# Four images through a four-layer network: LSTMs in pairs of images, all sampling moved behind the first pair

## The reference

```
x = x + L0(gn(x))   # attention of 8x8 blocks over 14x14 halo windows, 4 heads
x = x + L1(gn(x))   # LSTM, 128 hidden, along the 96 columns of each of the 96 rows; then a linear map to 32 channels
x = x + L2(gn(x))   # deformable 3x3 convolution: 9 bilinear samples per pixel at learned offsets, masked, convolved
x = x + L3(gn(x))   # each 8x8 block multiplied from both sides by one 8x8 matrix
```

## Time and profile before

| | us |
|---|---|
| three runs | 5402.57, 5425.98, 5408.45 (median 5408.45) |
| the profiled execution | 5414.31 |
| its span (first to last instruction) | 5412.5 |

### The profile page before, as it was taken

How to read it: one execution, slowest core, us unless ns; L and a number is a source line. 1 busy time by engine, 2 the same in 40 slices (tenths; PEclk the granted TensorE clock), 3 DMA queues, 4 the chain that set the end, 5 groups by cost and what they waited for, 6 DMA issues and landing times.

```text
span 5412.5 us, 63956 instructions
## 1 busy us (share of the span) xinstructions
PE 2775.3 (51%) x24896; PEld 2286.7 (42%) x24896; DVE 2142.2 (40%) x4277; ACT 1054.6 (19%) x2365; POOL 2550.1 (47%) x2615
## 2 busy tenths in 40 slices
PE   6877735665566624666566642666566651000001
PEld 4767624454556513544465522454356541000001
DVE  5632244443433434444333353444343353222222
ACT  4622212221211202222211211222221110000000
POOL 1000064445355564444455565444355456777774
PEclk9855565555555655655555575556555575555555
DMA  5510024332211214332111123333121121111111
GB/s 170 147 31 1 1 80 126 97 115 52 58 36 38 77 44 124 109 106 73 53 44 36 39 80 110 98 112 90 44 55 38 35 77 54 52 50 47 47 47 40
DMA packets 191156, 369.96 MB, mean 68 GB/s; under 512 B 58864, under 2 KB 88688, under 8 KB 190848
## 3 DMA queue, kind: packets, MB, share of 16 engines
q0 software_dynamic: 82944, 170.04, 12.1%
q1 hardware_dynamic: 104952, 192.41, 11.8%
q10 hardware_dynamic: 2960, 3.44, 0.2%
HBM read 260.46 MB, written 104.33 MB: 67 GB/s over the span
## 4 chain that ended last, share of the span: by engine, by line
PE 27%; issue 26%; DVE 18%; POOL 12%; another core or an unknown queue 10%; ACT 5%; DMA 1%; SPq 0%; ACTq 0%; DVEq 0%; POOLq 0%
POOL got L525 12%; PE bank L1366 8%; PE bank L1287 5%; DVE got L802 3%; PE bank L1272 2%; PE bank L1258 2%; DVE red L804 2%; DVE prod L1040 2%; ACT sig L676 2%; PE bank L1222 2%; DVE mx L876 2%; PE bank L1235 2%; DVE gc L1044 1%; PE bank L1187 1%
## 5 line engine op out<-in xcount | busy, mean ns | idle before, releaser
L525 POOL DMA_INDIRECT got<-sample_table,index x2592 | 2536.6, 979 | 2797.5 <-DVE red L804 1280.0
L1366 PE MATMUL bank<-hist,whh 128*128 128x96 f32 x3040 | 756.7, 429 | 554.3 <-DVE hist L1046 414.5
L1366 PEld LDWEIGHTS bank<-hist,whh 128*128 128x128 f32 x3040 | 667.9, 323 | 644.4 <-DVE hist L1046 475.4
L1187 PE MATMUL bank<-turned,wout 128*128 128x192 f32 x864 | 234.4, 443 | 902.2 <-DVE turned L810 625.3
L802 DVE TENSOR_TENSOR got<-got,weight 128x1152 f32<-128x1152 f32 x288 | 389.8, 1353 | 660.1 <-DMA got<-sample_table,index 659.8
L1187 PEld LDWEIGHTS bank<-turned,wout 128*128 128x128 f32 x864 | 216.0, 275 | 916.4 <-DVE turned L810 596.7
L876 DVE TENSOR_REDUCE mx<-bank 128x2 f32<-128x392 f32 x576 | 298.9, 557 | 690.0 <-remote 428.9
L608 ACT ACTIVATE pt<-bank 98x512 f32<-98x512 f32 x576 | 336.3, 596 | 1040.6 <-remote 564.1
L1040 DVE TENSOR_TENSOR prod<-sig,gc 128x192 f32<-128x192 f32 x384 | 135.5, 353 | 992.6 <-ACT sig L676 535.6
L1287 PE MATMUL bank<-pt,v 98*16 98x64 f32 x9216 | 366.4, 277 | 313.5 <-issue 310.8
L1287 PEld LDWEIGHTS bank<-pt,v 98*16 98x16 f32 x9216 | 222.9, 120 | 443.8 <-issue 421.5
(11 more groups left out here) (128 smaller groups left out, 3194.3 us busy)
## 6 DMA issues: line engine op xcount, KB each, us to landing
kst<-k_parts SPq DMA_DIRECT2D x96, 441.0 KB
got<-sample_table,index POOLq DMA_INDIRECT x2592
qst<-q_parts SPq DMA_DIRECT2D x96, 288.0 KB
k_parts<-kp SPq DMA_DIRECT2D x24, 882.0 KB
k_parts<-kp SPq DMA_DIRECT2D x24, 588.0 KB
q_parts<-qp SPq DMA_DIRECT2D x24, 576.0 KB
sample_table<-tab SPq DMA_DIRECT2D x8, 1568.0 KB
q_parts<-qp SPq DMA_DIRECT2D x24, 384.0 KB
```

The costliest lines, as they stand in the source:

```text
L525: pool.indirect_dma_start(out=got[:, uu % RING, n, :], out_offset=None, in_=tables[p], in_offset=bass.IndirectOffsetOnAxis(ap=at, axis=0)) ...
L1187: mm = pe.matmul(out_ps[k % 2], wout[:, tap, :], turned[:, k % 2, tap, :], start=(tap == 0), stop=(tap == NTAP - 1))
L1366: mm = pe.matmul(dst, whh[:, w], hist[:, (t - 1) % HIST, :], start=False, stop=True, skip_group_check=True)
```

## The change

```diff
-STAGES = (("l3", 4, 4), ("pre", 6, 7), ("l0", 3 * NU, 31), ("l1", W, 60), ("prep", 8, 64))
+    stages = ((2 * (6 + 3 * NU) + W + TABLE_POINTS + 3, 0),
+              (6 + 3 * NU, 42), (TABLE_POINTS + 3, 52),
+              (6 + 3 * NU, 92), (NT + 1, 95), (W, 130), (TABLE_POINTS + 3, 139),
+              (REST[0], 139 + REST[0]), (NT + 1, 156), (TABLE_POINTS, 160), (1, 161), (REST[1], 161 + REST[1]), (1, 170),
+              (REST[2], 170 + REST[2]), (1, 196), (REST[3], 196 + REST[3]), (NT + 1, 230), (REST[4] - FLUSH, B * UNITS), (FLUSH, B * UNITS))
+TABLE_POINTS = 4
+FLUSH = 8
+REST = (13, 8, 25, 30, 58 + FLUSH)
...
-GUNITS = 6
+GUNITS = NCOL
+ADDS = 2
+SLOTS2 = 4
...
-        x = sb("x", [P, 2, XR, W])
+        x = sb("x", [P, B, XR, W])
-            v = sb("v", [HKEYS, 2, NB * 2, J, HEADS, 2 * D], where=a0)
+            v = sb("v", [HKEYS, 2, NB * 2, J, HEADS, D + 1], where=a0)
...
             def prepare(p):
-                sp.wait_ge(lin_added, W // LIN * (p + 1))
+                for a in range(2):
+                    sp.wait_ge(lin_added[a], W // LIN * (p // 2 + 1))
+                wait(sp, tab_stored, 16 * len(TSTORES) * p)
+                sp.wait_ge(x_added, 2 * NG * ATTENDED[p])
+                sp.dma_start(base[:, :, :, :].rearrange("p m u n -> p (m u n)"), pix_base).then_inc(base_in, 16)
+                sp.dma_start(cw[:, :, :].rearrange("p t o -> p (t o)"), conv_w).then_inc(taps_in, 16)
...
                 for t in range(W):
-                    act.wait_ge(g_done, tt + 1)
-                    wait(act, prods_done, tt)
-                    act.activation(gc[:, 0, :], g_ps[t % 2][:, 0:W], ACT.Tanh).then_inc(g_act, 1)
-                    act.wait_ge(ifo_done, tt + 1)
-                    wait(act, hid_done, tt)
-                    act.activation(sig[:, :], ifo_ps[t % 2][:, 0:3 * W], ACT.Sigmoid).then_inc(ifo_act, 1)
-                    act.wait_ge(cell_done, tt + 1)
-                    act.activation(tcell[:, :], gc[:, 1, :], ACT.Tanh).then_inc(tanh_done, 1)
+                    for a in range(2):
+                        act.wait_ge(g_done[a], tt + 1)
+                        wait(act, prods_done[a], tt)
+                        act.activation(gc[:, a, 0, :], gates[a][:, h:h + W], ACT.Tanh)
+                        act.wait_ge(ifo_done[a], tt + 1)
+                        wait(act, hid_done[a], tt)
+                        act.activation(sig[:, a, :, :], gates[a][:, GATE_I:GATE_I + 6 * W].rearrange("p (g n) -> p g n", g=3)[:, :, h:h + W],
+                                       ACT.Sigmoid).then_inc(ifo_act[a], 1)
+                        act.wait_ge(cell_done[a], tt + 1)
+                        act.activation(tcell[:, a, :], gc[:, a, 1, :], ACT.Tanh).then_inc(tanh_done[a], 1)
...
                 for t in range(W):
-                    if t > 0:
-                        recurrence(t)
-                    if t + 1 < W:
-                        inputs(t + 1)
-                    if t % LIN == 0 and t > 0:
-                        linear(t // LIN - 1)
-                    point(p)
+                    for a in range(2):
+                        if t > 0:
+                            recurrence(a, t)
+                        if t % LIN == 0 and t > 0:
+                            linear(a, t // LIN - 1)
+                        if a == 0 and t % 2 == 0 and t > 0:
+                            inputs(1, t)
+                        if a == 1 and t % 2 == 1 and t + 1 < W:
+                            inputs(0, t + 1)
+                    point()
```

More of the change, by code:

```diff
@@ L43 @@
 LIN = 4
+GATE_I = 512 - 2 * W
 HIST = 8
@@ L443, in attention, with sequence_parts @@
                         store_k(p, G + 2, 2)
-            def sequence_parts(p):
+            def sequence_parts(pair):
                 for k, (first, last) in enumerate(CHUNKS):
[L447 to L452, removed]
-                                     x_parts[:, piece, first:last, :].rearrange("(j c) t f -> c j (t f)", j=J)).then_inc(xs_in[k], 16)
@@ L751, in transform @@
                     evacuate(r)
-            for q in range(B):
-                if q >= 2:
-                    transform(q - 2)
-                attention(q)
-                lstm(q)
-                prepare(q)
-            transform(B - 2)
-            transform(B - 1)
+            attention(0)
+            attention(1)
+            lstm(0)
+            prepare(0)
+            attention(2)
+            prepare(1)
+            attention(3)
+            transform(0)
+            lstm(1)
+            prepare(2)
+            transform(1)
+            prepare(3)
+            transform(2)
+            transform(3)
         @block.vector
@@ new lines, in point, with points @@
+            def point():
+                nonlocal point_count, units_done, adds_done
+                i = point_count
+                point_count += 1
+                while units_done < DUE[i]:
+                    unit(units_done)
+                    units_done += 1
+                while adds_done < B * NADD and ADD_AT[adds_done] <= i:
+                    add_rows(adds_done)
+                    adds_done += 1
+            def points(n):
+                for i in range(n):
+                    point()
@@ L1059, in prepare @@
+                for a in range(2):
+                    add_linear(W // LIN - 1, a)
             def prepare(p):
@@ L1366, in recurrence @@
[L1366 to L1371 removed]
+                        mm = pe.matmul(gate(a, n)[:, h:h + W], whh[:, w], hist[:, a, (t - 1) % HIST, :], start=False, stop=True,
+                                       skip_group_check=True)
@@ L1395, in prepare @@
+                    point()
+                for a in range(2):
+                    pe.wait_ge(hid_done[a], W * (pair + 1))
+                    linear(a, W // LIN - 1)
             def prepare(p):
```

681 lines of the change are left out of this document (365 added, 316 removed).

## The result

Against the kernel before on the same chip (5405.5 us median there), the changed kernel takes 5263.5 us, median of 4 runs (5237.8 to 5273.9): a ratio of 0.9725, interval 0.968 to 0.977. The forecast was 5160 in 4750 to 5480. So it is faster, by 2.7% and not by 4.6%.

A forecast was written before the change was run, and what follows sets the result against it. No engine was busy much over half, so a chain of stages was taken to set the time. First gather at 1121 us, second LSTM's end at 3257, then 1854 of units and 48 of end gave 5160 us, range 4750 to 5480.

The forecast's parts named there:

- the first gather as late as forecast: Start of the kernel up to GpSimd's first gather: forecast at 1121 us, 703 before the change.
- The pair's step: LSTM of two images at once: 5.5 us per t at the low clock, 528 us for 96 steps.
- The first rival: Both LSTMs: the pair raises the clock, ScalarE's order binds at 3.7 us per t, 4835 us in all; chance 0.22.
- the slower rival: Both LSTMs: the images don't overlap, 7.74 us per t, 5610 us in all; chance 0.15.
- the two loops without units: Loops of attention 0 and 1, with no sampling in them: 192 us each.
- The attention loops: Attention 2 and 3, 39 and 37 units: 500 and 490 us, from 7.2 matmuls per us during gathers.
- the third rival: Attention 2 and 3: a unit costs 10.8 us however dense, loops 613 and 592, 5375 us in all; chance 0.10.
- Units in the second LSTM: LSTM of images 2 and 3, 35 units: 48 us of convolutions and 47 of VectorE, stage 653 with its start.
- The rest: Behind the second LSTM: 152 units at 12.2 us, 1854 us without GpSimd waits, then 48 us of the end.
- such a wait would prove me wrong: Sign of error: GpSimd waits for VectorE or an index after the second LSTM.
- Named at nothing: Parts priced at no time, among them 3 MB more image loads beside the first projections, 20 us if uncovered.
- the summary behind the sum: Closing account of gains: 268 us of LSTM 0 and 1, 275 of the second pair, 370 of attention 1, mostly given back.

The follow-up runs named there:

- the filled kernel: Kernel before with twelve extra matmuls, read by nobody, in each LSTM step where TensorE would wait for the hidden state: 4148.3 us, ratio 0.9552.
- the run without gathers: Changed kernel with every unit's nine gathers replaced by one small GpSimd memset, sampling left out of the result: 3006.9 us, one run.

## Why the forecast was right, and where not

The sign was right on the chip that the forecast was made for, and the time 104 us too low. That was partly luck. With the first gather as late as forecast and everything behind it as measured the time would be some 5160 + 276 = 5436 us (an estimate), no gain over 5408. So the sign held only because the term that mattered most was wrong the other way. On the experiments' chips the same change is no gain, and nothing in the forecast would have told so.

**The pair's step** was the mis-sized term: 5.5 us per t taken, 3.55 measured. I took the low clock, since at the high one TensorE would be engaged for 75%, about the share at which the trace of before showed 0.5. That premise failed: the rows of the first LSTM have TensorE busy for 292.57 of 367 us at 0.50 and, filled, for 213.79 of 284 at 0.99, so a like busy share doesn't mean the low clock. The first rival was right on this point: clock 0.99, and 3.55 us where it had 3.7 (that ScalarE's order is what binds there was not tested). By the Trainium skill, "TensorE: Matmul & The Clock Gate", Part 1, the throttle is the default and sustained activity releases it; the filled kernel agrees (0.50 to 0.99 with nothing changed but twelve matmuls a step). The images do overlap: the slower rival is out. This gave (5.5 - 3.55) x 96 = 187 us. Attention took 23 of them: the LSTM began at 573 and not at 550, for the two loops without units took 206 and 210 us instead of 192 each (32 us, less 9 around them). 6 us came back in `prepare`, which leaves the 170.

**The attention loops** were to take 500 and 490 us, from a rate of matmuls during gathers. They took 592 and 577. That sum had GpSimd gathering nearly all the time. The loop got 3565 / 592 = 6.0 matmuls per us, not 7.3, and GpSimd waited 170 us in it for VectorE (181 in the loop before). With 37 units on record in it, a unit cost (592 - 210) / 37 = 10.3 us, nearly the 10.8 of the third rival, which had 613 and 592 us. That gathers leave room for more matmuls than before was wrong on this chip; on the others a unit costs (293 - 190) / 23 = 4.5 us before and (385 - 195) / 36 = 5.3 after.

**Units in the second LSTM** were priced at 1.4 us of VectorE and 4 us a convolution. The stage took 649 us, 26 more than the forecast's 623 behind its start, though the pair's step alone was again 187 faster: with 341 for the pair, (649 - 341) / 35 = 8.8 us a unit, and (464 - 337) / 35 = 3.6 on the other chips. In the kernel before it was 3.3 and 0.8 ((388 - 367) / 28 there). The rows have VectorE busy for 96 of 367 us in the single LSTM and for 191 of 337 in the pair's, so a unit finds less idle time there. That this is the reason for the 3.6 is read from them and from the run without gathers (465 us, the same cost of a unit), and was not tested by itself; the first chip's 8.8 is not explained by it.

**The rest** was to run at 12.2 us a unit without waits. It ran faster, (5213 - 3235 - 187) / 153 = 11.7 us, but with 187 us of waits of GpSimd for VectorE (by its waits in that stretch), behind convolutions whose end came late. I had said that such a wait would prove me wrong: the 187 us, less some 63 that the faster pace gives back, are 124 of the 128, and the last 4 are the end (52 us, not 48).

**Named at nothing**: the 14 and 18 us more in the two attention loops stand beside 3 MB more of image loads, which by the forecast would be 20 us if nothing covered them. Whether they are the cause was not tested: on another chip the second of these loops took 195 us, but the LSTM began at 569 all the same.

**A wrong figure that no forecast hangs on**: the summary behind the sum has 268 us of gain for the first pair of LSTMs. Its own figures give 371 + 464 + 2 x 32 - 558 = 341.

**What stays open.** On the first chip something delays TensorE's instructions and the signals of its results from the first gather on, and in every profile from the four others it doesn't. It isn't only a matter of a gather in progress: the answer at 5390.29 came late though the last gather had begun at 5364.3. The waits and windows above are where the two profiles of the same kernel differ; a single gather of the changed kernel takes 993 ns in both. So why a unit costs 10 us there is not shown, and with it the reason of the 2.7% is open: the experiments show the account of the waits, and the price of each stage, for the other chips. Whether it is the chip or something beside the kernel was not tested, and couldn't be, since no run met it again.

## What to carry to other kernels

Where one engine has a fixed sum of work behind a first input, write the time as that engine's first wait, its work and its other waits, and price a reordering by what it does to the two waits; stage by stage sums hide that one pays for the other. If TensorE's granted clock stands at half in a stage that waits on a recurrence, try a few idle matmuls in the wait before restructuring: here they gave 4.5%, where the restructuring gave 2.7% on one chip and lost 0.6% on the other chip that timed it unedited. And take the kernel before again on another chip before a difference of a few per cent is believed to be the kernel's.

## What the runs showed of the hardware

- The same program took 5405 us on one chip and 4346 to 4349 on four others; the stages compared that have no gathers took the same on either. Before those runs I took the 10.8 us of a unit for a property of the kernel.
- Twelve matmuls of 96 columns, read by nobody, took the granted clock from 0.50 (1.2 GHz) to 0.99 (2.4 GHz) and made the step of the LSTM 23% shorter; four gave 0.63 and 7%.
- In the first chip's profile after, a matmul of 0.59 us was answered by VectorE 4.5 us after its start, and turns of samples waited up to 41.3 us; in the kernel before, the last convolution was answered after 20 us on the first chip and after 4.7 us on another. Waits put down to "remote" come to 1739 and 2789 us in the first chip's two profiles, and to none elsewhere.
